# Attention weighting with the latents stationary, row sums on GpSimd, and queries placed by DMA in a transformer-layer kernel

## The chip, the cores and the metric

The kernel runs on one core of a Trainium2 chip. The metric is device time in microseconds, the median of several executions, lower is better. One further execution was recorded by the hardware profiler; durations of single instructions come from it. TensorE is PE in the rows (PEld its weight loads), VectorE is DVE, ScalarE is ACT, GpSimd is POOL and SyncE, which only issues DMAs here, is SP.

## The reference

The layer takes x of shape (16, 512, 256), 16 sequences of 512 tokens, and returns x plus an attention output plus a feed-forward output, both computed from the normalised x. Cut to what matters:

```
xn = (x - mean) / sqrt(var + 1e-5)
q = (xn @ Wq.T)                                  # 8 heads of 64
kv_latent = xn @ Wkv_down.T                      # 64 wide
k, v = kv_latent @ Wk_up.T, kv_latent @ Wv_up.T  # 8 heads of 64
attn = softmax(q k^T / 8);  a = (attn @ v) @ Wo.T
gate, y = fp4_linear(xn, w_gate), fp4_linear(xn, w_up)   # 704 wide
f = fp4_linear(silu(gate) * y, w_down)
return x + a + f
```

`fp4_linear` rounds both operands in blocks of 16 to a grid of eight magnitudes, scaled by the largest magnitude of the block. All numbers are float32 and every result must be close to float32.

## The kernel before, in words

Weights are folded once: Wk_up into Wq (`wqk`), Wv_up into Wo (`wov`). Each head then works on the 64-wide latents themselves: the scores are folded query times latent, and the weighted sum is a sum of latents (`lat_tok`, tokens on partitions, with a column of ones behind the 64 latents in which the sum of the weights appears). Most products split each operand into a rounded float32r part and a float32r remainder and do three matmuls (`limbs`, line 774). The product of probabilities and latents is not split. It is plain float32, and the trace records each such matmul as two matmuls with a weight load each; they are called halves here. The program that is built has 2,048 of these matmuls, the trace has 4,096.

The steady part is a loop of 128 slots, one for each head of each sequence, written out by hand for each engine; LEAD slots before it prepare and quantise weights, TAIL slots after it drain. In slot t, PE does: the gate product of a 128-token chunk and half of the 704 columns into bank `m0`; two of four maxima matmuls (`mx`, query chunk against all keys) for head t+2; a transpose of the row maxima of head t+1 (line 928); the up product into `m1`; key scores of head t (`st`, two matmuls each, lines 889 and 890, the second adds the query remainder and minus the row maximum); the transposes of the quantised hidden chunk of slot t-2 (line 876); the weighting matmuls (`weigh`, line 904: probabilities of 128 keys by 128 queries as the stationary operand, 65 columns of `lat_tok` as the moving one, 16 matmuls for a head); the down product of slot t-2. Every second slot adds the folded query of a pair of heads, or the transposes of a token chunk, or of a pair of normalised head outputs (`on`, line 1016). Once in a sequence of eight slots come the latents, their transposes (line 1024), and the output product `wov` in two halves. One PSUM bank, `m2`, takes all transposes. The outputs of a head lie with queries on partitions, so DVE divides them by the sum per partition (lines 675, 680), and PE turns them afterwards.

ACT does the tanh of the gate, the exponentials (line 506, one for each 128 keys of a head), and the rounded copies out of PSUM, among them four 64-partition copies of a query pair (line 546). DVE does the row maxima (line 611), the elementwise steps of the hidden chunk, the block scales (lines 583 to 588), the power of two of each value by two bit operations (`to_grid`, lines 593 and 595), the remainders, and the sums into `acc`. POOL does three elementwise steps for each hidden chunk and each token chunk. SP issues the loads of x, the stores and one 2 KB transfer for each head. Each engine works through its own list in order and waits on semaphores, so a late instruction holds everything behind it on its engine. `QH` is 4: queries of two pairs are held at a time.

## Time and profile before

| what | us |
|---|---|
| median of 3 runs | 1689.79 |
| lowest, highest | 1688.26, 1696.55 |
| the profiled execution, its own time | 1696.03 |
| its span, first to last instruction | 1694.0 |

The page gives for each engine the time it was busy in the span. A busy PE is not PE at its peak, because matmuls overlap and their recorded ends are modelled: the distance from one start to the next tells what a matmul costs. The chain of waits goes back from the last instruction, at each step to what released it or to the instruction ahead of it on its engine; a stretch of the chain that stays on PE is one in which PE had no gap. The granted clock of PE is a share of its full clock: 1.00 is 2.4 GHz, 0.50 is 1.2 GHz.

### The profile page before, as it was taken

To read this page: it belongs to the slowest core of one execution; us is meant where nothing else is said; L and a number is where in the kernel's file an instruction comes from. 1 tells how busy PE (TensorE), PEld (TensorE's weight loads), DVE (VectorE), ACT (ScalarE), POOL (GpSimd) and SP (SyncE) were. 2 spreads that over 40 slices of the span, in tenths; PEclk is the share of its full clock that TensorE was granted. 3 is DMA by queue.
4 is the path that set the end of the run, shared out by engine and by line. 5 is a ranking of instruction groups with operands and counts; after the bars stand their busy time and mean duration, and the time that the engine had idled before them with its cause. 6 is when DMAs were issued, how large, how long until landed. Compare 5 with 4: busy or idle time off the path is not lost.

```text
span 1694.0 us, 30412 instructions
## 1 busy us (share of the span) xinstructions
PE 1577.0 (93%) x10726; PEld 1442.1 (85%) x10726; DVE 1340.1 (79%) x3368; ACT 708.9 (42%) x1382; POOL 517.8 (31%) x696
## 2 busy tenths in 40 slices
PE   0599999999999999999999999999999999999998
PEld 0488998989889898988989899898989989898897
DVE  8788787888888888888878788878888877787663
ACT  2444444444444444444443444444344444344432
POOL 7433232332232233323223323223233322332211
PEclk9799999999999999999999999999999999999999
DMA  3000000000000000000000000000000000000000
GB/s 98 7 10 4 8 20 4 19 8 11 14 8 17 7 20 7 10 14 7 17 7 20 4 14 14 8 17 7 20 5 14 14 4 20 7 11 8 1 14 13
DMA packets 22885, 22.60 MB, mean 13 GB/s; under 512 B 3280, under 2 KB 22224, under 8 KB 22736
## 3 DMA queue, kind: packets, MB, share of 16 engines
q1 hardware_dynamic: 22736, 20.65, 4.0%
q8 instruction: 89, 1.46, 0.4%
q14 instruction: 60, 0.49, 0.1%
HBM read 11.99 MB, written 8.39 MB: 12 GB/s over the span
## 4 chain that ended last, share of the span: by engine, by line
PE 87%; DVE 9%; issue 3%; ACT 1%; DMA 0%; POOL 0%; SPq 0%; DVEq 0%; POOLq 0%
PE m L774 35%; PE po L904 23%; PE mx L863 7%; PE st L889 7%; PE st L890 6%; PE m L876 3%; PE m L1010 2%; PE m L1016 1%; PE m L928 1%; DVE row_max L611 1%; PE m L1024 1%; DVE hid L595 1%; DVE on_lo L745 1%; DVE h_small L583 1%; DVE x_small L583 1%
## 5 line engine op out<-in xcount | busy, mean ns | idle before, releaser
L904 PEld LDWEIGHTS po<-lat_tok,probs 128*128 128x128 f32 x4096 | 523.5, 194 | 22.9
L904 PE MATMUL po<-lat_tok,probs 128*128 128x65 f32 x4096 | 519.1, 270 | 0.0
L506 ACT ACTIVATE probs<-st 128x512 f32<-128x512 f32 x512 | 291.3, 595 | 338.2 <-PE st L890 338.2
L611 DVE TENSOR_REDUCE row_max<-mx 128x1 f32<-128x512 f32 x512 | 327.7, 682 | 0.6 <-PE mx L863 0.6
L411 POOL TENSOR_TENSOR h_norm<-hid,h_small 128x352 f32<-128x352 f32 x128 | 100.8, 788 | 480.7 <-DVE h_small L588 480.7
L889 PE MATMUL st<-q_hi,lat 128*128 128x512 f32 x512 | 212.7, 415 | 0.0
L890 PE MATMUL st<-q_lo,lat 65*128 65x512 f32 x512 | 203.6, 398 | 0.0
L774 PE MATMUL m<-wgu_hi,xt_hi 128*128 128x352 f32 x512 | 191.9, 375 | 0.1
L724 DVE TENSOR_TENSOR q_lo<-m,q_hi 64x512 fp32r<-64x512 f32 x128 | 88.1, 688 | 122.4 <-ACT q_hi L546 122.4
L442 POOL TENSOR_TENSOR h_norm<-h_norm,hid 128x352 f32<-128x352 f32 x128 | 119.7, 935 | 211.6 <-DVE h_norm L597 211.6
L863 PE MATMUL mx<-lat,q_hi 128*128 128x512 f32 x512 | 176.5, 426 | 4.0 <-DVE row_max L611 3.9
L546 ACT ACTIVATE q_hi<-m 64x512 fp32r<-64x512 f32 x256 | 151.5, 592 | 64.0 <-PE m L774 59.3
L774 PE MATMUL m<-wgu_lo,xt_hi 128*128 128x352 f32 x512 | 169.5, 331 | 0.0
L774 PE MATMUL m<-wgu_hi,xt_lo 128*128 128x352 f32 x512 | 168.4, 329 | 0.0
L526 ACT ACTIVATE ht_hi<-m 128x384 fp32r<-128x384 f32 x128 | 62.8, 491 | 198.5 <-PE m L876 198.5
L657 DVE TENSOR_TENSOR ht_lo<-m,ht_hi 128x384 fp32r<-128x384 f32 x128 | 71.3, 557 | 67.4 <-ACT ht_hi L526 67.4
L774 PEld LDWEIGHTS m<-wgu_hi,xt_hi 128*128 128x128 f32 x512 | 100.7, 197 | 14.0 <-issue 4.6
L514 ACT ACTIVATE hid<-m 128x352 f32<-128x352 f32 x128 | 59.4, 464 | 125.1 <-PE m L774 121.7
L774 PE MATMUL m<-wd_hi,ht_hi 128*128 128x256 f32 x384 | 107.7, 280 | 1.3 <-DVE ht_lo L657 1.3
L774 PE MATMUL m<-wd_hi,ht_lo 128*128 128x256 f32 x384 | 107.0, 279 | 0.0
L774 PE MATMUL m<-wd_lo,ht_hi 128*128 128x256 f32 x384 | 106.9, 278 | 0.0
L411 POOL TENSOR_TENSOR hq<-h_norm,h_small 128x352 f32<-128x352 f32 x128 | 100.7, 787 | 10.0
(178 smaller groups left out, 3054.2 us busy)
## 6 DMA issues: line engine op xcount, KB each, us to landing
x_in<-in_L_attn_x_dram SPq DMA_DIRECT2D x64, 128.0 KB, 2.2
out_dram<-acc SPq DMA_DIRECT2D x32, 256.0 KB, 2.3
q_lo<-neg_max SPq DMA_DIRECT2D x128, 2.0 KB
weights_in<-in_L_ffn_w_down_dram SPq DMA_DIRECT2D x1, 704.0 KB, 6.3
weights_in<-in_L_ffn_w_gate_dram SPq DMA_DIRECT2D x1, 640.0 KB, 4.7
acc<-in_L_ffn_w_up_dram SPq DMA_DIRECT2D x1, 640.0 KB, 5.9
wq_in<-in_L_attn_Wq_dram SPq DMA_DIRECT2D x1, 512.0 KB, 5.9
x_in<-in_L_attn_Wo_dram SPq DMA_DIRECT2D x1, 512.0 KB, 7.0
```

The costliest lines, as they stand in the source:

```text
L411: return pool.tensor_tensor(blocks(dst), blocks(src), per_block.unsqueeze(2).broadcast_to([rows, cols // BLOCK, BLOCK]), ALU.mult)
L442: pool.tensor_tensor(h_norm[:, :], h_norm[:, :], hid[:, w.c % 2, :], ALU.subtract).then_inc(h_grid, 1)
L506: act.activation(probs[:, t.c % 2, kc, :], st[kc % 2][:, :], ACT.Exp).then_inc(exp_done, 1)
L546: act.activation(q_hi[v * R:(v + 1) * R, 2 * m.c % QH + u, :], m1[u * R:(u + 1) * R, :], ACT.Copy).then_inc(q_hi_done, 1)
L611: dve.tensor_reduce(row_max[:, u.c % 2, qc:qc + 1], mx[qc % 2][:, :], AX.X, ALU.max).then_inc(mx_taken, 1)
L657: dve.tensor_tensor(ht_lo[:, u.c % 2, :, :], m2[:, 0:NB * P].rearrange("p (k q) -> p k q", k=NB), ht_hi[:, u.c % 2, :, :].bitcast(F32), AL ...
L724: dve.tensor_tensor(q_lo[0:R, h, :], m1[v * R:(v + 1) * R, :], q_hi[v * R:(v + 1) * R, h, :].bitcast(F32), ALU.subtract).then_inc(q_lo_don ...
L774: last = pe.matmul(dst, a, b, start=(n == 0), stop=(n == len(ms) - 1))
L863: pe.matmul(mx[qc % 2][:, :], q_hi[:, u.c % QH, qc * P:(qc + 1) * P], lat[:, s.c % 2, :], start=True, stop=True).then_inc(mx_psum, 1)
L889: pe.matmul(st[kc % 2][:, :], lat[:, s.c % 2, keys], q_hi[:, h, :], start=True, stop=False)
L890: pe.matmul(st[kc % 2][:, :], lat1[:, s.c % 2, keys], q_lo[:, h, :], start=False, stop=True).then_inc(st_psum, 1)
L904: last = pe.matmul(po[:, qc * P:qc * P + R + 1], probs[:, u.c % 2, kc, qc * P:(qc + 1) * P], lat_tok[:, s.c % 2, kc, 0:R + 1], start=(kc = ...
```

## The change

- **The weighting product is turned round.** The 64 latents of 128 keys are now stationary, and the 512 probabilities of those keys for all queries stream. The two heads of a pair go to partitions 0 to 63 and 64 to 127 of `po`, that is, to two column tiles of the array. There are 8 such matmuls for a pair of heads, done together in one even slot, where there were 32 of 65 columns.
- **The sums.** GpSimd adds the probabilities of the four key chunks of a head (`add_keys`, three additions of 128x512). TensorE then multiplies the sum tiles with a column of ones: 16 matmuls for a pair, each with 64 stationary columns of the sum tile taken 8 elements apart, and one moving column. DVE takes reciprocals (128x8). They lie on other partitions than needed, so SP writes them to DRAM and reads them back spread over the partitions (`inv_b`).
- **The head outputs** come out already turned, so the transposes of `on` go. DVE scales a pair with one multiplication, ACT rounds it, GpSimd takes the remainder (before, DVE).
- **Queries.** ACT rounds a pair with one 128-partition copy and DVE takes one remainder, where there were four copies and two remainders. SP places the results with six transfers a pair.
- **Grid rounding** of the hidden and token chunks: two ACT operations (square, then a bf16 copy with a bias) replace two DVE bit operations.
- **Down product**: the two halves of a chunk accumulate in one group of 18 matmuls every second slot; x is loaded a second time, into `acc`, as what it is added to.
- **Order** within a slot is new on all engines; the latent transposes go to `m1`; LEAD has 14 slots (12), TAIL 6 (4).

The diff, cut to its core:

```
-        def turned_pair(t):
+        def weighed_pair(t):
             m = t.plus(-2).over(2)
             return m if t.c % 2 == 0 and m.within(B * PAIRS) else None
+        def scaled_pair(t):
+            m = t.plus(-3).over(2)
+            return m if t.c % 2 and m.within(B * PAIRS) else None
+        def split_pair(t):
+            return weighed_pair(t.plus(-2))
...
+        def down_chunk(t):
+            n = t.plus(-5).over(2)
+            return n if t.c % 2 and n.within(B * CH) else None
         def wov_half(t):
             s = t.over(H).plus(-1)
-            m = s.times(2, t.c % H - 1)
-            return m if t.c % H in (1, 2) and m.within(B * 2) else None
-        LEAD = [At(c) for c in range(-12, 0)]
-        TAIL = [At(SLOTS + c) for c in range(4)]
+            m = s.times(2, t.c % H - 2)
+            return m if t.c % H in (2, 3) and m.within(B * 2) else None
+        LEAD = [At(c) for c in range(-14, 0)]
+        TAIL = [At(SLOTS + c) for c in range(6)]
...
+            def place_query(m, u):
+                h = 2 * m.c % QH + u
+                sp.wait_ge(q_hi_done, m.n(1, 1))
+                if u and m.over(2).any():
+                    sp.wait_ge(st_psum, m.n(2 * CH, -2 * CH))
+                for v in range(2):
+                    sp.dma_start(q_hi[v * R:(v + 1) * R, h, :].bitcast(F32), qp_hi[u * R:(u + 1) * R, :].bitcast(F32)).then_inc(q_hi_placed[u], 16)
+                sp.wait_ge(q_lo_done, m.n(1, 1))
+                sp.dma_start(q_lo[0:R, h, :].bitcast(F32), qp_lo[u * R:(u + 1) * R, :].bitcast(F32)).then_inc(q_lo_placed[u], 16)
...
+                m = scaled_pair(t)
+                if m is not None:
+                    sp.wait_ge(inv_done, m.n(1, 1))
...
+                if m is not None:
+                    sp.wait_ge(inv_stored, m.n(16, 16))
+                    for v in range(2):
+                        sp.dma_start(inv_b[v * R:(v + 1) * R, :],
+                                     inv_rows[m.c % 2, v:v + 1, :].broadcast_to([R, T])).then_inc(inv_spread, 16)
...
+                m = q_pair(t)
+                if m is not None:
+                    place_query(m, 0)
...
+            def add_keys(t, kc):
+                total, last = key_sum[:, t.c % 2, :], probs[:, t.c % 2, kc, :]
+                pool.wait_ge(exp_done, t.n(CH, kc + 1))
+                if kc == 1:
+                    if t.over(2).any():
+                        pool.wait_ge(den_psum, t.over(2).n())
+                    first = probs[:, t.c % 2, 0, :]
+                else:
+                    pool.wait_ge(sum_step, t.n(CH - 1, kc - 1))
+                    first = total
+                pool.tensor_tensor(total, first, last, ALU.add).then_inc(sum_step, 1)
...
                 if w.within(SLOTS):
-                    pool.wait_ge(h_round, w.n(ROUND_STEPS, ROUND_STEPS))
+                    add_keys(w, 3)
+                m = split_pair(t)
+                if m is not None:
+                    pool.wait_ge(on_hi_done, m.n(1, 1))
+                    pool.tensor_tensor(on_lo[:, m.c % PAIRS, :], on[:, :], on_hi[:, m.c % PAIRS, :].bitcast(F32),
+                                       ALU.subtract).then_inc(on_lo_done, 1)
...
+                if t.within(SLOTS):
+                    add_keys(t, 1)
+                    add_keys(t, 2)
...
+                    act.wait_ge(h_norm_done, w.n(1, 1))
+                    act.activation(hid[:, w.c % 2, :], h_norm[:, :], ACT.Square, scale=MAGIC_SQUARE).then_inc(h_square, 1)
+                    act.wait_ge(h_square, w.n(1, 1))
+                    act.activation(h_magic[:, :], hid[:, w.c % 2, :], ACT.Copy, bias=MAGIC_LEAST).then_inc(h_magic_done, 1)
+                n = norm_chunk(w)
...
+                m = split_pair(t)
+                if m is not None:
...
+                m = q_pair(t)
+                if m is not None:
...
-                m = q_pair(t)
-                if m is not None:
-                    act.wait_ge(q_psum, m.n(1, 1))
-                    if m.any(2 * CH, -2 * CH):
-                        act.wait_ge(st_psum, m.n(2 * CH, -2 * CH))
-                    for u in range(2):
...
+                max_rows(t, 0)
+                max_rows(t, 1)
...
+                m = scaled_pair(t)
+                if m is not None:
+                    dve.wait_ge(inv_spread, m.n(32, 32))
+                    dve.wait_ge(pv_done, m.n(CH, CH))
+                    if m.any():
+                        dve.wait_ge(on_hi_done, m.n())
+                        dve.wait_ge(on_lo_done, m.n())
+                    dve.tensor_tensor(on[:, :], po[:, :], inv_b[:, :], ALU.mult).then_inc(on_done, 1)
+                m = q_pair(t)
+                if m is not None:
+                    dve.wait_ge(q_hi_done, m.n(1, 1))
...
+                m = weighed_pair(t)
+                if m is not None:
+                    dve.wait_ge(den_psum, m.n(1, 1))
+                    if m.any(1, -1):
+                        dve.wait_ge(inv_stored, m.n(16, -16))
...
-            def weigh(t, n):
-                u, kc = (t.plus(-1), n + 2) if n < 2 else (t, n - 2)
-                if u.within(SLOTS):
-                    s = u.over(H)
-                    if kc == 0:
-                        if u.any():
-                            pe.wait_ge(on_done, u.n())
-                        pe.wait_ge(ltok_done, s.n(1, 1))
-                    pe.wait_ge(exp_done, u.n(CH, kc + 1))
-                    for qc in range(CH):
-                        last = pe.matmul(po[:, qc * P:qc * P + R + 1], probs[:, u.c % 2, kc, qc * P:(qc + 1) * P],
-                                         lat_tok[:, s.c % 2, kc, 0:R + 1], start=(kc == 0 and qc == 0),
-                                         stop=(kc == CH - 1), skip_group_check=True)
...
+            def weigh(t):
+                m = weighed_pair(t)
+                if m is not None:
+                    s = m.over(PAIRS)
+                    if m.any():
+                        pe.wait_ge(on_done, m.n())
+                    pe.wait_ge(ltok_done, s.n(1, 1))
+                    for kc in range(CH):
+                        pe.wait_ge(exp_done, m.n(2 * CH, CH + kc + 1))
+                        for v in range(2):
+                            last = pe.matmul(po[v * R:(v + 1) * R, :], lat_tok[:, s.c % 2, kc, 0:R], probs[:, v, kc, :],
+                                             start=(kc == 0), stop=(kc == CH - 1))
+                        last.then_inc(pv_done, 1)
...
+            def weights_sum(t):
+                m = weighed_pair(t)
+                if m is not None:
+                    s = m.over(PAIRS)
+                    if t.plus(-2).within(SLOTS) or t.plus(1).within(SLOTS):
+                        turned_taken(t)
+                    else:
+                        m2_free(t.plus(-1))
+                    pe.wait_ge(sum_step, m.n(2 * (CH - 1), 2 * (CH - 1)))
+                    for j in range(T // R):
+                        for v in range(2):
+                            last = pe.matmul(m2[v * R:(v + 1) * R, j:j + 1],
+                                             key_sum[:, v, :].rearrange("p (q j) -> p q j", j=T // R)[:, :, j],
+                                             lat_tok[:, s.c % 2, 0, R:R + 1], start=True, stop=True)
+                    last.then_inc(den_psum, 1)
...
-                                           wgu_lo[:, k, cols]) for k in range(KD)]).then_inc(up_psum, 1)
+                if wov_half(t.plus(-1)) is None:
+                    gate(t)
+                    up(t)
+                else:
+                    up(t)
+                    gate(t)
+                turn(t)
+                weigh(t)
                 key_scores(t, 0)
-                turn_hidden(t)
-                weigh(t, 0)
                 key_scores(t, 1)
-                weigh(t, 1)
+                if q_pair(t) is not None:
...
-                                       for k in range(NB)]).then_inc(down_psum, 1)
+                weights_sum(t)
                 key_scores(t, 2)
                 key_scores(t, 3)
```

What TensorE's list has between the transposes of a hidden chunk and the next maxima matmuls, before (in the program itself; each `po` row stands for twice as many records of the trace):

```order
L876 MATMUL m<-ident,hq 128x128 x3
L904 MATMUL po<-lat_tok,probs 128x65 x4
L889 MATMUL st<-q_hi,lat 128x512
L890 MATMUL st<-q_lo,lat 128x512
L904 MATMUL po<-lat_tok,probs 128x65 x4
L863 MATMUL mx<-lat,q_hi 128x512 x2
```

And in an even slot of the changed kernel (`m` of line 1052 is bank m2):

```order
L987 MATMUL m<-ident,hq 128x128 x3
L991 MATMUL m<-ident,row_max 4x128
L1036 MATMUL po<-probs,lat_tok 64x512 x8
L1003 MATMUL st<-q_hi,lat 128x512
L1004 MATMUL st<-q_lo,lat 128x512
L1003 MATMUL st<-q_hi,lat 128x512
L1004 MATMUL st<-q_lo,lat 128x512
L975 MATMUL mx<-lat,q_hi 128x512 x2
L1052 MATMUL m<-lat_tok,key_sum 64x1 x16
```

The four weighting groups of every slot have become one group of eight long matmuls in every second slot, and the 16 short ones stand behind the maxima.

SP's list over three slots, before:

```order
L384 DMA out_dram<-acc 128x2x256
L376 DMA q_lo<-neg_max 1x4x128
L384 DMA out_dram<-acc 128x2x256
L351 DMA x_in<-in_L_attn_x_dram 128x256
L376 DMA q_lo<-neg_max 1x4x128 x2
```

And now, over an even and an odd slot:

```order
L423 DMA q_lo<-neg_max 1x4x128
L453 DMA acc<-in_L_attn_x_dram 128x256
L419 DMA inv_rows<-inv_den 128x8
L423 DMA q_lo<-neg_max 1x4x128
L428 DMA inv_b<-inv_rows 64x512 x2
L409 DMA q_hi<-qp_hi 64x512 x2
L411 DMA q_lo<-qp_lo 64x512
L382 DMA x_in<-in_L_attn_x_dram 128x256
L409 DMA q_hi<-qp_hi 64x512 x2
L411 DMA q_lo<-qp_lo 64x512
```

The store and the two spreads of the reciprocals stand round the transfer of the negated maxima, ahead of the queries.

GpSimd's list over one slot, before:

```order
L442 TENSOR_TENSOR h_norm<-h_norm,hid 128x352
L411 TENSOR_TENSOR hq<-h_norm,h_small 128x352
L458 TENSOR_TENSOR rstd<-rstd,minus_half 128x1
L411 TENSOR_TENSOR h_norm<-hid,h_small 128x352
L411 TENSOR_TENSOR x_norm<-xn,x_small 128x256
```

And now, in an even slot:

```order
L516 TENSOR_TENSOR key_sum<-key_sum,probs 128x512 x2
L526 TENSOR_TENSOR on_lo<-on,on_hi 128x512
L533 TENSOR_TENSOR h_norm<-h_norm,h_magic 128x352
L481 TENSOR_TENSOR hq<-h_norm,h_small 128x352
L549 TENSOR_TENSOR rstd<-rstd,minus_half 128x1
L481 TENSOR_TENSOR h_norm<-hid,h_small 128x352
L481 TENSOR_TENSOR x_norm<-xn,x_small 128x256
L516 TENSOR_TENSOR key_sum<-probs 128x512
```

Key sums and a remainder of 512 columns have come in around the steps of the hidden chunk.

## Rows read from the trace of the kernel before

**Rows 1.** The page's part 1: span, busy time and share, instructions

```profile
span 1694.0 us, 30412 instructions
PE 1577.0 (93%) x10726; PEld 1442.1 (85%) x10726; DVE 1340.1 (79%) x3368; ACT 708.9 (42%) x1382; POOL 517.8 (31%) x696
```

**Rows 2.** The page's part 4: the chain that ended last, by engine

```profile
PE 87%; DVE 9%; issue 3%; ACT 1%; DMA 0%; POOL 0%; SPq 0%; DVEq 0%; POOLq 0%
```

**Rows 3.** Line 514, the tanh, one for each slot: min/median/max ns, first and last start

```profile
L514 ACT ACTIVATE hid<-m x128: 459/464/467, 91.5 to 1664.7; 128x352 f32<-128x352 f32 x128
```

**Rows 4.** The chain, 800 to 826 us: start us, length us, what

```profile
800.24 1.40 PE m L774 x6
...
806.64 1.02 PE m L774 x6
807.65 0.46 PE mx L863 x2
808.11 0.11 PE m L928
808.22 0.96 PE m L774 x6
...
809.42 0.23 PE st L890
...
812.69 1.06 PE m L774 x9
...
814.69 0.84 PE po L904 x8
815.53 2.79 PE m L774 x24
818.32 0.44 PE m L1016 x4
```

**Rows 5.** The timeline, PE, 96 to 98 us: start, length, what

```profile
96.14 1.90 PE L904 MATMUL po<-lat_tok,probs 128*128 128x65 f32 x16
97.84 0.41 PE L774 MATMUL m<-wgu_hi,xt_hi 128*128 128x352 f32 x1
```

**Rows 6.** The timeline, PE, 53.5 to 57 us: plain float32, 256 columns

```profile
53.59 1.92 PE L822 MATMUL st<-weights_in 128*128 128x256 f32 x4
55.30 1.91 PE L822 MATMUL po<-weights_in 128*128 128x256 f32 x4
```

**Rows 7.** Busy time by stretches: PE, PEld, DVE, ACT, POOL, then PE clock

```profile
53.40:57.00 3.60, 3.60 (x10) 2.79 (x9) 1.05 (x2) 1.19 (x2) 1.07 (x2) 0.50 0.00 0
93.00:140.00 47.00, 45.77 (x304) 41.02 (x303) 43.23 (x108) 21.17 (x42) 16.44 (x22) 1.00 0.02 7
90.00:890.00 800.00, 769.99 (x5274) 704.99 (x5274) 653.58 (x1641) 345.17 (x669) 242.19 (x322) 0.99 0.04 11
```

**Rows 8.** The chain, 800 to 899 us: pieces that are not PE's work

```profile
866.49 0.61 DVE on_lo L745
...
884.53 0.43 issue
```

**Rows 9.** Lines 442 and 451, POOL, two inputs from SBUF: min/median/max ns

```profile
L442 POOL TENSOR_TENSOR h_norm<-h_norm,hid x128: 925/932/952, 100.3 to 1671.4; 128x352 f32<-128x352 f32 x128
L451 POOL TENSOR_TENSOR x_norm<-x_norm,xq x64: 722/733/752, 14.3 to 1526.8; 128x256 f32<-128x256 f32 x64
```

**Rows 10.** Groups of instructions by line: busy us, mean ns | idle before

```profile
L724 DVE TENSOR_TENSOR q_lo<-m,q_hi 64x512 fp32r<-64x512 f32 x128 | 88.1, 688 | 122.4 <-ACT q_hi L546 122.4
L595 DVE TENSOR_SCALAR hid<-hid 128x352 f32<-128x352 f32 x128 | 66.6, 520 | 4.4
L546 ACT ACTIVATE q_hi<-m 64x512 fp32r<-64x512 f32 x256 | 151.5, 592 | 64.0 <-PE m L774 59.3
```

**Rows 11.** DMA issues (KB each, us to landing) and SP's queue in the timeline

```profile
x_in<-in_L_attn_x_dram SPq DMA_DIRECT2D x64, 128.0 KB, 2.2
...
821.53 0.58 SPq L376 DMA_DIRECT2D q_lo<-neg_max  x1
```

More of the change, by code:

```diff
@@ L208, in transformer_layer @@
         q_lo_done = sem("q_lo_done")
+        q_hi_placed = [sem(f"q_hi_placed{b}") for b in range(2)]
+        q_lo_placed = [sem(f"q_lo_placed{b}") for b in range(2)]
         mx_psum = sem("mx_psum")
@@ L236, in transformer_layer @@
         down_taken = sem("down_taken")
+        res_loaded = [sem(f"res_loaded{c}") for c in range(CH)]
         wov_psum = sem("wov_psum")
@@ L327, in lead_work @@
         def lead_work(t):
-            i = t.c + len(LEAD)
+            i = t.c + 12
+            if i < 0:
+                return range(0), range(0)
             quants = (min(2 * i, len(WQUANT)), min(2 * i + 2, len(WQUANT)))
@@ L553, in slot @@
                                    ACT.Copy).then_inc(xt_hi_done, 1)
-                m = turned_pair(t)
-                if m is not None:
-                    act.wait_ge(on_psum, m.n(1, 1))
-                    if m.over(PAIRS).any(2):
-                        act.wait_ge(wov_psum, m.over(PAIRS).n(2))
-                    act.activation(on_hi[:, m.c % PAIRS, :], m2[:, :], ACT.Copy).then_inc(on_hi_done, 1)
                 s = ltok_seq(t)
@@ new lines, in slot @@
+                if m is not None:
[9 more added lines that the diff above has]
+                    if m.any():
+                        for u in range(2):
+                            dve.wait_ge(q_lo_placed[u], m.n(16))
+                    dve.tensor_tensor(qp_lo[:, :], m1[:, :], qp_hi[:, :].bitcast(F32), ALU.subtract).then_inc(q_lo_done, 1)
@@ L909, in slot, with into_hidden @@
[L909 to L920 removed]
+            def into_hidden(t, dst, first, done):
+                s, c, j = t.over(H), t.c % H // 2, t.c % 2
+                b, tok, cols = s.c % 2, slice(c * P, (c + 1) * P), slice(first + j * HALF, first + (j + 1) * HALF)
+                limbs(dst[:, 0:HALF], [(xt_hi[:, b, KD + k, tok], xt_lo[:, b, KD + k, tok], wgu_hi[:, k, cols],
+                                        wgu_lo[:, k, cols]) for k in range(KD)]).then_inc(done, 1)
@@ L944, in slot @@
+                m = q_pair(t)
+                if m is not None:
+                    b, cols = m.over(PAIRS).c % 2, slice(m.c % PAIRS * P, (m.c % PAIRS + 1) * P)
+                    limbs(m1[:, :], [(wqk_hi[:, k, cols], wqk_lo[:, k, cols], xt_hi[:, b, k, :], xt_lo[:, b, k, :])
+                                     for k in range(KD)]).then_inc(q_psum, 1)
+                d = down_chunk(t)
+                if d is not None:
                     if t.within(SLOTS):
```

345 lines of the change are left out of this document (171 added, 174 removed).

## The prediction

> **What bounds the kernel now.** I read the page's part 1 first: PE is busy for 93% of the span, DVE for 79%, POOL for 31% [rows 1]. A busy share of PE proves little, so the chain of waits came next: 87% of it is PE, 9% DVE [rows 2], and most of that 9% is the preparation before the first slot. The tanh is done once in each slot, so its first and last start give the period: (1664.7 - 91.5) / 127 = 12.39 us a slot [rows 3]. Between 800 and 826 us the chain does not leave PE at all [rows 4]. So the slots are bound by how long TensorE takes for its list; gaps come in a few places.
>
> How much is list and how much is gap, for a pair of slots (24.77 us)? From the pieces of the chain [rows 4]: four gate and up products of about 1.0 are 4.0; eight maxima matmuls at 0.23 are 1.9; sixteen score matmuls at 0.235 are 3.8; eight single transposes at 0.11 are 0.9; eight weighting groups at 0.84 are 6.7; two down products 2.1; a query product 1.4; two groups of four transposes 0.9. A sequence of four pairs adds two output products of 2.8, and the latents and their transposes (1.4 and 0.44), 1.9 for a pair. The sum is 23.6. So 1.2 us of a pair are gaps. Two of them show: DVE's work for the transpose bank `m2` before the latents can be turned, and short waits ahead of the row maxima [rows 8].
>
> **What a plain float32 matmul costs.** This decides everything. At the 1.2 GHz level (granted clock 0.50 [rows 7]) four halves of 256 columns take 55.30 - 53.59 = 1.71 us [rows 6], 0.428 each, which is 513 clocks: a half streams a column in two clocks. At 2.4 GHz (clock 1.00 [rows 7]) sixteen halves of 65 columns take 97.84 - 96.14 = 1.70 us [rows 5], 0.106 each, while 65 columns would stream in 0.054. So the weighting matmuls of before are bound by what comes with a half, the load of 128 stationary columns, and not by streaming.
>
> **The change, part by part**, for a pair of slots.
> - Weighting, removed: 64 halves at 0.105 = -6.7 us. Transposes of `on`, removed: -0.44 [rows 4].
> - Weighting, added: 8 matmuls, 16 halves of 512 columns. Each streams 1024 clocks, 0.427 us at 2.4 GHz; the float32r matmuls of 512 columns take 0.235 [rows 4] where 512 clocks are 0.213, 10% more, so the bounds are 0.427 and 0.47, and I take 0.45. The load is hidden behind the stream. No row shows two column tiles at work. If the tiles do not overlap, all 16 halves stand in a row: 7.2 us. If they overlap, the order is two halves on tile A, two on tile B; the second half of one runs beside the first of the other, and the group takes 9 halves: 9 x 0.45 = 4.05. I take 4.05 and keep 7.2 for the range. The Trainium skill says in "TensorEngine Tiling (Array Packing)", section Key Properties, that different tiles can load weights and multiply in parallel, and that a change of the tiling mode drains the engine; no run so far shows the first here.
> - Mode changes, added: four for a pair. The nearest row is the transpose with four stationary columns between 128-wide ones, 0.11 like other transposes [rows 4], so nothing to 0.3 us each; I take 0.3 in all.
> - Sums of the weights, added: 16 matmuls, 32 halves with 64 stationary columns and one moving column. No row shows one. From above the half with 128 stationary columns bounds it, 0.106: 3.4 us. From below, if the two tiles load side by side, a quarter: 0.8. Half the columns at the same rate are 0.053; with something for issue I take 0.06, 1.9 us.
> - Gaps: the latents' transposes leave `m2`, the transposes of `on` are gone, and the row-maxima transpose comes after gate and up; the waits of [rows 8] go. What is late next is DVE in the odd slot: it must wait for the spread reciprocals, scale the pair, take the query remainder and the down product, and only then does the maxima 2 and 3 which the next slot's first matmuls need. I let 0.6 of the 1.2 us remain; bounds 0 and 1.8.
> - POOL: two-input steps take 0.932 for 352 and 0.733 for 256 columns [rows 9], 2.07 ns a column, so 512 columns take 1.26. Three key sums a slot and half a remainder are 4.4 us beside the 242.19 / 800 x 12.39 = 3.75 of now [rows 7]: 8.2 us of a slot of 11.6. That hides, and it costs if the slot falls under 8.2 or each addition grows above 2.2 us.
> - DVE: 653.58 / 800 x 12.39 = 10.1 us a slot now [rows 7]. It loses the bit operations (line 595 alone 0.52 [rows 10]), one of two query remainders (0.69 a pair [rows 10]), the remainder of `on` (0.61 [rows 8]), the small division. Some 2 us less a slot, none of it directly on the path, since PE was.
> - ACT: 345.17 / 800 x 12.39 = 5.3 us now. Four query copies of 0.592 [rows 10] become one; up to 1.4 us of squares and copies come in. It stays under 6.2 us, hidden.
> - SP: nine more issues for a pair, and one load of 128 KB again. At 0.58 an issue [rows 11] about 13 issues take 7.5 us of 23, hidden in bulk. In order it matters: the spread waits behind the negated maxima, which appear about 3.3 us into the odd slot. Two issues (1.2) and a landing like that of x (2.2 [rows 11]) give 6.7 us; DVE, by its list, comes there at about 6.8. The queries' first half must be there at the next slot's start: rounded at about 6, placed at 9.3, in a slot of about 11. Both are close and cost nothing as long as a small DMA lands in about 2 us.
>
> The sum for a pair: -6.7 - 0.44 + 4.05 + 0.3 + 1.9 - 0.6 = -1.5 us, from 24.8 to 23.3. Times 64: -96 us. TAIL has the store and the spread on its path, LEAD two more slots in which nothing waits: +4 (0 to 10). Against the profiled execution, 1696.0 - 96 + 4 = 1604. That execution was 6.2 us above the median of the runs, so the median should be about 1598; I say 1600.
>
> **The rivals.**
> - *The column tiles do not overlap.* The group takes 16 halves, 7.2 us, and the pair grows by 3.15: +202 us, of which the longer even slot gives DVE and SP time and hides perhaps 10. About 1790, slower by 6%. Its place is line 1036, and it decides as soon as the group takes over 5.6 us (4.05 + 1.5). For it: no row of before shows overlap, and two streams of float32 must be read at once. Against it: each half takes a column only every second clock, so both together need no more than one float32r stream reads.
> - *The small loads are slow.* The sums' stationary tile is read 8 elements apart. If this halves the rate of the load, a half costs 0.106 as with 128 columns, the sums take 3.4 us and not 1.9: +96, about 1695, no change to slightly slower. Every stationary operand in the rows is read without a step, so they neither exclude nor show it. The same holds if 0.106 is the cost of issue and not of 128 columns. The Trainium skill's "SBUF — State Buffer", section Door 1, has the rule that speaks for it: lines of 16 bytes, and a penalty for each access that moves to a new line, which 32-byte steps always do.
> - *The reciprocals come late.* DVE waits in every odd slot for the DRAM round trip. Each microsecond beyond 6.8 us into the slot delays query remainder, down product and maxima, and so the next slot: 64 us for each. With landings of 3 us instead of 2.2, on the store and on the spread, about +1: 1665. For it: SP issues in order behind two waits. Against it: the store is issued early in the slot, well before the maxima.
>
> **How the numbers follow.** Forecast 50% (1600, its own range 1545 to 1665), tiles apart 24% (about 1790), slow loads 16% (about 1695), late reciprocals 10% (about 1665). What this measurement can tell from no change is about 0.5%, 8 us. Faster by more: nearly all of the forecast, a quarter of the slow loads, two thirds of the late reciprocals, 0.58. Within it 0.07. Slower: the tiles apart, half of the slow loads, 0.35. The range runs from 1545 to 1790; it holds the first, third and fourth case and half of the second.
>
> **What would show it.** In the changed profile the eight matmuls of line 1036 should lie 0.85 to 0.95 us apart for a pair of heads and the group should hold PE for about 4 us; 7 us means that the tiles stand in a row. Line 1052's 32 halves should take about 2 us; 3.4 means slow loads. The tanh's period should be near 11.65 us. DVE should wait little for `inv_b` at line 793. POOL should be near 70% busy and not appear on the chain. The forecast is wrong if the chain runs through POOL or SP, or if line 1036 takes more than 5.6 us.

## The result and the profile after

The changed kernel takes 1681.51 us (median of 8 runs, 1671.57 to 1689.08) against 1691.01 us for the kernel before on the same chip (8 runs); the ratio is 0.994, 95% interval 0.9914 to 0.9966. I had forecast 1600 us. The measured time lies in the range, but of a gain of 91 us only about 10 came. The profiled execution took 1683.32 us, with a span of 1681.5.

The page's parts 1, 2 and 4 of the changed kernel:

```profile
span 1681.5 us, 28756 instructions
...
PE 1561.3 (93%) x9446; PEld 1217.2 (72%) x9446; DVE 1167.5 (69%) x2664; ACT 716.8 (43%) x1574; POOL 1068.4 (64%) x1144
...
PEclk9689999999999999999999999999989999998998
...
PE 71%; DMA 9%; DVE 7%; ACT 5%; issue 3%; SPq 3%; POOL 1%; POOLq 0%; DVEq 0%; ACTq 0%
PE m L875 28%; PE po L1036 13%; PE mx L975 8%; PE m L1052 8%; DMA inv_b<-inv_rows 6%; PE st L1003 6%; PE st L1004 4%; DMA q_hi<-qp_hi 3%; PE m L987 2%; DVE qp_lo L800 1%; SPq L423 1%; DVE row_max L717 1%; SPq L428 1%; ACT probs L602 1%; ACT neg_max L618 1%
```

Against [rows 1] PE is as busy as before, 93%, with 1280 fewer matmul records and 225 us less weight loading. A list that I reckoned 1.5 us a pair shorter keeps the engine busy for nearly as long. Against [rows 2] the chain has a new part, DMA 9% and SP's queue 3%, where both were 0%. So there are two places to look for the lost gain: why TensorE needs so long for a shorter list, and what the transfers hold up.

The tanh of each slot, line 610 now (first and last start at the end of the times):

```profile
L610 ACT ACTIVATE hid<-m x128: 463/463/467, 96.5 to 1646.7; 128x352 f32<-128x352 f32 x128
```

The period is (1646.7 - 96.5) / 127 = 12.21 us, where [rows 3] gave 12.39 and I expected 11.65. A pair of slots takes 24.41 us: 0.36 less than before, not 1.5 less.

The chain of waits of the changed kernel over a pair (start us, length us, what):

```profile
787.63 0.64 SPq L423
...
788.32 0.51 SPq L428
...
788.88 2.96 DMA inv_b<-inv_rows
...
791.87 0.06 DVE on L793
...
792.47 0.68 DVE qp_lo L800
...
797.60 3.58 PE po L1036 x16
...
802.78 2.02 PE m L1052 x32
...
805.93 4.37 PE m L875 x24
...
814.70 4.17 DMA inv_b<-inv_rows
```

Read it from its three ends. The 16 halves of line 1036 hold PE for 3.58 us: the column tiles do overlap. The 32 halves of the sums take 2.02. And then, behind four score matmuls, the output product, 24 matmuls of 256 columns, takes 4.37 us, where the same product took 2.79 in [rows 4] (the row at 815.53). Nothing in its instructions has changed. In the timeline of PE its matmuls start 0.12 us apart, then 0.21, then 0.12 again:

```profile
802.71 2.09 PE L1052 MATMUL m<-lat_tok,key_sum 128*64 128x1 f32 x32
...
805.89 0.28 PE L875 MATMUL m<-wov_lo,on_hi 128*128 128x256 f32 x1
806.00 0.28 PE L875 MATMUL m<-wov_hi,on_lo 128*128 128x256 f32 x1
...
807.11 0.41 PE L875 MATMUL m<-wov_hi,on_lo 128*128 128x256 f32 x1
807.32 0.41 PE L875 MATMUL m<-wov_hi,on_hi 128*128 128x256 f32 x1
...
809.77 0.28 PE L875 MATMUL m<-wov_hi,on_hi 128*128 128x256 f32 x1
809.89 0.28 PE L875 MATMUL m<-wov_lo,on_hi 128*128 128x256 f32 x1
```

The windows of the same kernel (busy time of PE, PEld, DVE, ACT, POOL, then the granted clock) show why. The second stretch ends with the score matmuls, the third holds most of the output product:

```profile
802.00:806.00 4.00, 4.00 (x42) 3.40 (x41) 2.37 (x7) 1.47 (x4) 2.01 (x3) 1.00 0.01 1
806.00:810.00 4.00, 4.00 (x23) 4.00 (x22) 0.29 (x3) 0.58 (x2) 3.28 (x4) 0.57 0.01 0
810.00:816.00 6.00, 5.65 (x32) 4.72 (x31) 4.35 (x8) 3.23 (x9) 1.74 (x2) 1.00 0.05 17
...
100.00:1600.00 1500.00, 1451.15 (x8854) 1129.67 (x8853) 1062.98 (x2388) 655.35 (x1438) 977.68 (x1023) 0.94 0.23 59
```

The burst of short matmuls ends at 804.8. From about 806.2 on the clock is at 0.50, the 1.2 GHz level, for 3.4 us, and PE is busy all the time. Over 100 to 1600 us the mean is 0.94. The kernel before in the same stretch:

```profile
100.00:1600.00 1500.00, 1449.73 (x9940) 1329.74 (x9939) 1210.98 (x3026) 642.13 (x1244) 448.26 (x592) 0.98 0.04 11
```

A mean of 0.98 is 1500 x 0.02 x 2 = 60 us at the lower level, 0.94 is 180 us. Of the 120 us more, half is lost, since each microsecond there does half the work: about 60 us (the two decimals leave it open by 15 or so).

Not every burst does this. The trace of the changed kernel has 61 bursts between 100 and 1600 us and 45 falls of the clock. Of these, 38 begin between 0.5 us before and 1.7 us behind the end of a burst, with no gap of TensorE over 0.15 us in the 8 us ahead of them; they hold 147 of the 171 us at the lower level. The other seven begin around 2 us behind the start of an idle stretch of 1.3 to 2.1 us. The kernel before has nine falls over the same stretch, and all nine stand at such an idle stretch (1.4 to 2.1 us, TensorE waiting for DVE ahead of the transposes of the latents), as here, with columns as above:

```profile
865.00:866.00 1.00, 0.01 (x1) 0.00 (x0) 0.93 (x3) 0.60 (x1) 0.62 (x1) 1.00 0.00 0
866.00:867.00 1.00, 0.00 (x0) 0.00 (x0) 1.00 (x2) 0.00 (x0) 0.43 (x1) 0.74 0.00 0
867.00:868.00 1.00, 0.85 (x4) 0.86 (x5) 0.09 (x1) 0.00 (x0) 0.92 (x2) 0.50 0.00 0
```

So the clock falls here behind two different things: a wait of TensorE, and a burst of short matmuls during which it counts as busy.

The waits of the changed kernel on the new transfers and the new tilings (total us, times, longest), and the landings of its DMAs (KB each, us):

```profile
PEld po L1036 <- issue: 123.6, 447, 0.3
...
PEld st L1003 <- issue: 51.3, 64, 0.8
...
PEld mx L975 <- DMA q_hi<-qp_hi: 41.2, 43, 2.4
...
DVE on L793 <- DMA inv_b<-inv_rows: 26.1, 34, 2.3
```

```profile
q_hi<-qp_hi SPq DMA_DIRECT2D x256, 128.0 KB, 2.3
...
inv_b<-inv_rows SPq DMA_DIRECT2D x128, 128.0 KB, 2.9
...
inv_rows<-inv_den SPq DMA_DIRECT2D x64, 4.0 KB, 1.4
```

### The profile page after: what moved, and what is told of

The parts are those of the page before. It is cut to its first block, busy times and chain, and to the rows that moved or that the text cites. A ratio compares the mean times of both kernels' runs of the same rounds, so it can differ in the third digit from the quotient of the medians.

```text
span 1681.5 us, 28756 instructions
## 1 busy us (share of the span) xinstructions
PE 1561.3 (93%) x9446; PEld 1217.2 (72%) x9446; DVE 1167.5 (69%) x2664; ACT 716.8 (43%) x1574; POOL 1068.4 (64%) x1144
## 3 DMA queue, kind: packets, MB, share of 16 engines
q8 instruction: 77, 1.26, 0.3%
## 4 chain that ended last, share of the span: by engine, by line
PE 71%; DMA 9%; DVE 7%; ACT 5%; issue 3%; SPq 3%; POOL 1%; POOLq 0%; DVEq 0%; ACTq 0%
PE m L875 28%; PE po L1036 13%; PE mx L975 8%; PE m L1052 8%; DMA inv_b<-inv_rows 6%; PE st L1003 6%; PE st L1004 4%; DMA q_hi<-qp_hi 3%; PE m L987 2%; DVE qp_lo L800 1%; SPq L423 1%; DVE row_max L717 1%; SPq L428 1%; ACT probs L602 1%; ACT neg_max L618 1%
## 5 line engine op out<-in xcount | busy, mean ns | idle before, releaser
L516 POOL TENSOR_TENSOR key_sum<-key_sum,probs 128x512 f32<-128x512 f32 x256 | 329.2, 1286 | 38.7 <-ACT probs L602 2.5
L1036 PE MATMUL po<-probs,lat_tok 128*64 128x512 f32 x1024 | 233.8, 598 | 0.0
L533 POOL TENSOR_TENSOR h_norm<-h_norm,h_magic 128x352 f32<-128x352 f32 x128 | 112.0, 875 | 154.7 <-DVE h_norm L774 154.7
L526 POOL TENSOR_TENSOR on_lo<-on,on_hi 128x512 fp32r<-128x512 f32 x64 | 82.8, 1293 | 196.2 <-ACT on_hi L643 196.2
L516 POOL TENSOR_TENSOR key_sum<-probs 128x512 f32<-128x512 f32 x128 | 163.5, 1277 | 8.9 <-PE m L1052 8.9
L1036 PEld LDWEIGHTS po<-probs,lat_tok 128*64 128x64 f32 x1024 | 67.8, 136 | 123.9 <-issue 123.6
L975 PEld LDWEIGHTS mx<-lat,q_hi 128*128 128x128 f32 x512 | 96.1, 204 | 82.9 <-DMA q_hi<-qp_hi 41.2
L1003 PEld LDWEIGHTS st<-q_hi,lat 128*128 128x128 f32 x512 | 100.7, 197 | 69.6 <-issue 51.3
L1052 PEld LDWEIGHTS m<-lat_tok,key_sum 128*64 128x64 f32 x2048 | 128.3, 216 | 24.6 <-issue 24.6
L1052 PE MATMUL m<-lat_tok,key_sum 128*64 128x1 f32 x2048 | 133.6, 259 | 0.9 <-POOL key_sum L516 0.9
L1004 PEld LDWEIGHTS st<-q_lo,lat 65*128 65x128 f32 x512 | 102.6, 200 | 14.9
```

Of the source, the lines that this page charges most:

```text
L516: pool.tensor_tensor(total, first, last, ALU.add).then_inc(sum_step, 1)
L526: pool.tensor_tensor(on_lo[:, m.c % PAIRS, :], on[:, :], on_hi[:, m.c % PAIRS, :].bitcast(F32), ALU.subtract).then_inc(on_lo_done, 1)
L533: pool.tensor_tensor(h_norm[:, :], h_norm[:, :], h_magic[:, :], ALU.subtract).then_inc(h_grid, 1)
L975: pe.matmul(mx[qc % 2][:, :], q_hi[:, u.c % QH, qc * P:(qc + 1) * P], lat[:, s.c % 2, :], start=True, stop=True).then_inc(mx_psum, 1)
L1003: pe.matmul(st[kc % 2][:, :], lat[:, s.c % 2, keys], q_hi[:, h, :], start=True, stop=False)
L1004: pe.matmul(st[kc % 2][:, :], lat1[:, s.c % 2, keys], q_lo[:, h, :], start=False, stop=True).then_inc(st_psum, 1)
```

## The experiments

Ratios are to the kernel before, run on the same chip, with their 95% intervals. The clock is the mean of the granted clock over 100 to 1600 us unless another stretch is named.

| kernel | us | ratio | clock |
|---|---|---|---|
| before | 1691.01 | 1 | 0.98 |
| changed | 1681.51 | 0.994 (0.9914 to 0.9966) | 0.94 |
| one of eight sum columns | 1503.56 | 0.8885 (0.8859 to 0.8911) | 1.00 (to 1500) |
| sums in four groups | 1676.15 | 0.9899 (0.9849 to 0.995) | 0.97 |
| spread issued first | 1647.75 | 0.9721 (0.9678 to 0.9763) | 0.95 |
| before, with a burst | 1926.19 | 1.1377 (1.1307 to 1.1447) | 0.92 |
| spread first, head 0 direct | 1649.91 | 0.9777 (0.9732 to 0.9821) | 0.93 (span) |
| ones stationary | 1615.61 | 0.9554 (0.954 to 0.9568) | 0.98 |
| four groups, spread first | 1657.28 | 0.9803 (0.9777 to 0.9828) | 0.97 (to 1500) |
| both heads on one tile | 1897.85 | 1.121 (1.1169 to 1.1251) | 0.94 (span) |
| ones stationary, reciprocal last | 1655.45 | 0.9813 (0.9784 to 0.9841) | 0.96 |
| ones stationary, in two halves | 1588.83 | 0.9422 (0.94 to 0.9445) | 0.99 |

**Is it the burst's own time or what it does to the clock?** Two kernels, one that takes the burst away and one that puts it elsewhere. The first computes one of the eight sum columns and leaves out the other seven, so the normalisation is not the reference's; all else stays.

```
-                    for j in range(T // R):
+                    for j in range(1):
...
-  dve.reciprocal(inv_den[:, m.c % 2, :], m2[:, 0:T // R])
+  dve.reciprocal(inv_den[:, m.c % 2, :], m2[:, 0:1].broadcast_to([P, T // R]))
```

> The changed kernel with 1 of the 8 columns of the sum matmuls (4 halves in place of 32; the reciprocals take that column 8 times, so the normalisation is left out). List theory: TensorE loses 28 halves of 0.063 us, 1.77 us a pair, 64 pairs: -113 us from 1681, about 1568. Clock theory: the burst of short matmuls is also what lowers TensorE's clock to the 1.2 GHz level for some 3.4 us in every second pair; then the granted clock rises from 0.93 to about 0.97 and another 60 us go: about 1508. If a wait behind the DRAM trip bounds the pair, less than 113 goes: above 1568.

Measured 1503.56. 28 of 32 halves are gone, 28 x 2.02 / 32 = 1.77 us a pair, 113 us in all. The gain is 178 us, so 65 us are not the burst's own time. That is less than the windows give: a mean of 0.94 over 1500 us is 90 us lost, this kernel loses under 10, and so some 80 came back. The rest may be waits that the lower clock had covered, or the two decimals; the runs do not tell. A window of this kernel shows the clock that came back:

```profile
700.00:1000.00 300.00, 291.02 (x1641) 219.88 (x1640) 245.82 (x556) 149.61 (x331) 227.50 (x237) 1.00 0.26 68
```

The second takes the kernel before and adds 32 halves of the same shape, on constant data and into unused columns of `m2`, in every second slot; nothing waits for their results.

```
+                    if t.c % 2 == 0:
+                        for n in range(8):
+                            for v in range(2):
+                                pe.matmul(m2[v * R:(v + 1) * R, NB * P + n:NB * P + n + 1],
+                                          x_const[:, v, :].rearrange("p (q j) -> p q j", j=8)[:, :, n],
+                                          ident[:, 0:1], start=True, stop=True)
```

> The kernel before with 16 idle plain float32 matmuls added in every second slot ahead of the down product, 64 stationary columns taken 8 apart and one moving column, results unused (the burst of the change, measured by itself in a list without other changes). List theory: 32 halves of 0.063 us and 0.3 for the change of tiling, 2.3 us a pair, +148 us: about 1838 and a mean clock of 0.97 as before. Clock theory: the clock falls behind the burst here too, another +60: about 1900, clock near 0.93.

Measured 1926.19. The burst in its chain, and one window of it:

```profile
801.38 2.02 PE m L956 x32
```

```profile
400.00:700.00 300.00, 292.77 (x2060) 268.17 (x2059) 207.34 (x525) 109.35 (x211) 77.86 (x103) 0.91 0.03 10
```

The list grows by 64 x 2.02 = 129 us, and the kernel before took 1694.44 on this chip, which makes 1824. The other 102 us are more than the list: over 100 to 1800 the mean of the clock is 0.924 (0.91 to 0.93 up to 1600 us, 0.96 behind that), 1700 x 0.076 = 129 us lost, less the 30 of before, 99. So the burst lowers the clock in a kernel that has nothing else of the change, and two different ways of counting agree within a few microseconds. Together with the kernel above this settles that the burst is the cause.

**Can the burst be spread out?** The eight columns in four groups of two, between the scores and the maxima:

```
                weigh(t)
+                weights_sum(t, 0)
                key_scores(t, 0)
                key_scores(t, 1)
+                weights_sum(t, 1)
...
-                weights_sum(t)
+                weights_sum(t, 2)
                key_scores(t, 2)
                key_scores(t, 3)
+                weights_sum(t, 3)
```

> The changed kernel with the 16 sum matmuls in four groups of four: behind the weighting group, behind key scores 1, behind the maxima matmuls, behind key scores 3. Same matmuls, same results. Clock theory: fewer stretches of short matmuls at once, the clock falls less often, -60 us, against which two or three more changes of the tiling stand with 0.3 us each for a pair, +40 to +50: about 1670, mean clock above 0.96. If the clock has another cause: clock unchanged at 0.93 and 1720 to 1730.

Measured 1676.15, with the changed kernel's interval overlapping. The clock rose from 0.94 to 0.97, as the theory of the clock wanted, which is 1500 x 0.03 = 45 us given back, and the time hardly moved. I had expected 1670 for this case, with a price of 40 to 50 us for more changes of the tile size. The first group stands behind the weighting group, which has the same tile size; each of the other three has a change ahead of it and one behind it. The waits show the place:

```profile
L1053 PEld LDWEIGHTS m<-lat_tok,key_sum 128*64 128x64 f32 x2048 | 148.8, 210 | 104.3 <-issue 104.3
```

The load sat idle 104.3 us ahead of the sums with the cause "issue", against 24.6 us in the changed kernel. Idle time of the load is not all lost, so this shows the place and a bound, not the sum; that the changes of tile size take the rest of the 45 us is argued.

**What does the late spread cost?** In SP's order the two spread transfers go ahead of the maxima's transfer, which waits for ACT:

```
+                if m is not None:
+                    sp.wait_ge(inv_stored, m.n(16, 16))
+                    for v in range(2):
+                        sp.dma_start(inv_b[v * R:(v + 1) * R, :], ...)
                 u = t.plus(1)
                 if u.within(SLOTS):
                     sp.wait_ge(neg_done, u.n(1, 1))
```

> The changed kernel with SP's two issues that spread the reciprocals moved ahead of the transfer of the negated maxima. Queue theory: the spread lands up to 2 us earlier in each odd slot, DVE's scaling and with it query remainder, down product and maxima are earlier; 1.0 to 1.5 us of a pair go, -64 to -96 us, about 1600. Clock theory alone: the gaps are covered anyway, -20 us or less, about 1665. If the negated maxima become late instead: no gain.

Measured 1647.75: 34 us less than the changed kernel, so the late spread was worth that much. In this kernel it is gone:

```profile
DVE on L792 <- DMA inv_b<-inv_rows: 3.5, 1, 3.5
```

It lies between the two expectations, 1600 and 1665, with the clock still at 0.95. Its chain shows what is late next, the rounded query behind ACT's work for the other streams:

```profile
823.87 0.50 ACT qp_hi L653
...
824.38 0.50 SPq L409
...
824.93 2.33 DMA q_hi<-qp_hi
...
827.30 0.94 PE mx L974 x2
```

So I let ACT write head 0's rounded query straight from PSUM into `q_hi`, and dropped its two transfers, on top of this order:

```
+  for v in range(2):
+      act.activation(q_hi[v * R:(v + 1) * R, 2 * m.c % QH, :], m1[0:R, :], ACT.Copy).then_inc(q_direct, 1)
...
-  for v in range(2):
+  for v in range(2 if u else 0):
```

> e3 (1648 us) and, for the first head of a pair, ACT writes the rounded query straight from PSUM in two 64-partition copies; only the second head's goes by DMA. In e3 the chain takes 6.9% in the landing of q_hi. Theory that the trip of the query is the next wait: its issue 0.5 and landing 2.3 go, two copies of 0.59 come, about 1 to 1.5 us in those odd slots that wait: -40 to -70, about 1595. Rival, ACT is late itself (its squares stand ahead of the exponentials) and the two copies delay the next exponentials: -10 or a loss.

Measured 1649.91, no gain. DMA and SP's queue left the chain (9% together with the spread in front, 0% now); in their place ACT went from 10% to 13%, DVE from 4% to 7% and issue from 3% to 5%. The expectation's rival, that ACT is late itself and two more copies delay it, fits, but the chain is that of the slowest execution, 1664.95, and no run holds ACT's delay alone.

The spread in front and the sums in four groups together:

> e2 and e3 together: the sum matmuls in four groups, the spread issued first. If the two causes are separate their gains add: 1681 - 33 - 5, about 1642. If a steadier clock only moves work into the waits of the odd slots, e3's gain grows with it, since with the spread early nothing is left to cover: 1600 to 1620.

Measured 1657.28. The gains do not add; the two together are slower than the spread alone, although the clock is at 0.97 and not at 0.95. What costs more than the clock gives back was not measured by itself; the three extra groups and their changes of tile size are all that differs.

**Do the two column tiles really run together?** Both heads go to column tile 0, head 1 on top of head 0, so that the weighted sums of the two heads are mixed; the instructions are the same in number and size.

```
-  last = pe.matmul(po[v * R:(v + 1) * R, :], ..., start=(kc == 0), stop=(kc == CH - 1))
+  last = pe.matmul(po[0:R, :], ..., start=(kc == 0 and v == 0), stop=(kc == CH - 1 and v == 1))
```

> The changed kernel with both heads' weighting matmuls on column tile 0 (their sums run together, the second tile's output is left out). Measures the overlap of the tiles. If the tiles overlap as the trace says (3.65 us for 16 halves), this takes 16 x 0.43 = 6.9 us a group: +3.2 us a pair, +205 us, about 1885, less what gaps absorb (up to 30) and less if the longer streaming holds the clock up. If the overlap in the trace is only in the modelled ends: no change.

Measured 1897.85. The group, in the chain:

```profile
812.57 7.01 PE po L1036 x16
```

7.01 us against 3.58, and (7.01 - 3.58) x 64 = 220 us against 216 measured. The overlap is nearly complete: a half is 0.438, and 16 of them on two tiles take the time of 8.2.

**Another way to the same sums.** A block of ones is stationary and the key sums are streamed, 4 halves of 512 columns for a pair; each of 64 rows then holds the sum, so the trip through DRAM goes, but DVE takes a reciprocal of 128x512.

```
-  for j in range(T // R):
-      for v in range(2):
-          last = pe.matmul(m2[v * R:(v + 1) * R, j:j + 1], key_sum[...][:, :, j], lat_tok[..., R:R + 1], ...)
+  for v in range(2):
+      last = pe.matmul(m2[v * R:(v + 1) * R, :], ones_w[:, :], key_sum[:, v, :], start=True, stop=True)
...
-  dve.reciprocal(inv_den[:, m.c % 2, :], m2[:, 0:T // R]).then_inc(inv_done, 1)
+  dve.reciprocal(inv_b[:, :], m2[:, :]).then_inc(inv_done, 1)
```

> The changed kernel with the sums taken by ones as the stationary operand (64 columns) and the summed probabilities streamed, 2 matmuls of 512 columns on the two column tiles, so that the sums come out spread over the partitions: no short matmuls, no DRAM trip; DVE takes one reciprocal of 128x512 in an even slot in place of 128x8. TensorE: 3 halves' time of 0.4 in place of 2.0, -50 us; clock theory: no fall behind it, -60; no wait for the spread, -30. DVE's reciprocals show about 5.9 ns a column beyond a base (0.207 us at 8, 0.289 at 22), so 512 columns would take about 3.1 us. If that hides on DVE (69% busy): about 1550. If DVE then bounds the pair, 1600 to 1680.

Measured 1615.61. The clock is back at 0.98. The reciprocal takes 3.36 us, which is 6.6 ns a column:

```profile
L806 DVE RECIPROCAL inv_b<-m 128x512 f32<-128x512 f32 x64 | 214.9, 3358 | 5.7 <-PE m L1042 5.7
```

DVE is now busy for 85% of the span and has 21% of the chain. Two orders on DVE followed. In the first the whole reciprocal stands behind the next chunk's scales and the latents' low part:

```
-  (weighed_pair) dve.reciprocal(inv_b[:, :], m2[:, :])      # ahead of xn and its scales
+  (weighed_pair) dve.reciprocal(inv_b[:, :], m2[:, :])      # behind lat
```

> As the streamed-ones kernel (1615.6 us), but VectorE's reciprocal of 128x512 stands behind the scales of the next x chunk and the low limb of the latents in its slot, not ahead of them. There the chain of waits of the streamed-ones kernel holds it: 3.13 us from 806.95 and then VectorE up to the latents' limb at 811.4. If it is the order on VectorE that costs, some 1 us of each 25 us pair comes back in the slots where the latents or the x chunk are waited for: about 1570 to 1600 us. Rival: VectorE is simply full (85% busy), so whatever stands last is late, and the turning of the next slot now waits for the reciprocal: 1610 to 1640 us.

Measured 1655.45: slower than either of the two expectations. It is the rival's mechanism at a higher price: the load and the transposes of the next slot wait for the bank that the reciprocal reads.

```profile
PEld m L978 <- DVE inv_b L824: 62.3, 34, 4.3
```

Part of the price is the clock, though this kernel has no burst of short matmuls. The kernel with ones stationary and this one, over the same stretch:

```profile
100.00:1600.00 1500.00, 1392.47 (x7439) 1007.91 (x7437) 1302.57 (x2456) 678.21 (x1490) 1023.12 (x1058) 0.98 0.20 49
100.00:1600.00 1500.00, 1385.19 (x7261) 1003.27 (x7259) 1240.45 (x2416) 662.65 (x1455) 993.40 (x1033) 0.96 0.20 49
```

The 0.02 are about 30 of the 40 us between them. All 24 falls of this kernel begin within 4.2 us of the start of an idle stretch of TensorE of 2.0 to 2.4 us.

In the second it is cut in two: 256 columns in the old place, 256 behind the latents' low part.

> As the one before, but the reciprocal is cut into two pieces of 256 columns, one in its old place and one behind the latents' limb. If order is what costs, it lands between: about 1590 to 1610 us; if the total of VectorE is the bound, it is no faster than 1615 us, plus about 0.1 us a pair for the second instruction, 6 us.

Measured 1588.83, the fastest of all and just ahead of what was expected, with the clock at 0.99:

```profile
L806 DVE RECIPROCAL inv_b<-m 128x256 f32<-128x256 f32 x64 | 112.5, 1758 | 5.7 <-PE m L1049 5.7
L831 DVE RECIPROCAL inv_b<-m 128x256 f32<-128x256 f32 x64 | 109.4, 1710 | 0.5
```

The second instruction costs (1758 + 1710 - 3358) = 110 ns, and the order gives back 27 us in all, 22 by the ratios. Other cuts were not tried.

## Why the prediction was wrong, step by step

- **What bounds the kernel.** Right: the slots were bound by TensorE's list, and the list of the changed kernel can still be counted from the same rows.
- **The tiles, "I take 4.05 and keep 7.2 for the range".** Right in kind, and a little too dear: 3.58 to 3.65 us instead of 4.05, 26 to 30 us in all in favour of the change. The experiment with one tile shows that the overlap is worth 216 us.
- **The sums, 1.9 us a pair.** Right: 2.02 to 2.09. The small loads are not slow; with a step of 8 elements in the stationary operand a half still takes 0.063 us, against 0.106 for 128 columns [rows 5]. The Trainium skill's "SBUF — State Buffer", section Door 1, which stood beside the rival of slow loads, has lines of 16 bytes and a penalty for each access that moves to a new one. By it a half would cost more than with adjacent elements; no row here has both, so a small price is not excluded. Half of 0.106 is 0.053, so it would be at most 0.01 us a half.
- **The failed step is the sum itself: "-6.7 - 0.44 + 4.05 + 0.3 + 1.9 - 0.6 = -1.5 us".** Every term of it takes the 2.4 GHz level for granted. I had used both levels to price a half [rows 6, 7], and then assumed that PE, always busy, would stay at the upper one. It does not: behind 2 us of matmuls with one moving column the clock fell in 38 of 61 pairs, mostly for 3.4 us. On average this takes about 1 us of each pair: 60 us in all against the kernel before by the windows, and the kernel with one sum column got 65 us back beyond its list. The term was put at nothing without a reason, and no rival held it. The forecast of the period was 23.3 us a pair and it came out at 24.4; the clock is the largest part of the difference.
- **"Both are close and cost nothing as long as a small DMA lands in about 2 us".** Wrong for the spread: it landed in 2.9 us, and in 4.17 in the next pair, not in 2.2, and SP took it up only behind the maxima's transfer; DVE stood idle for it in 34 of the 64 pairs, 0.8 us each time. This is my third rival, to which I gave 10%. It costs 34 us, and the order on SP's queue removes it. The rounded queries are late too (41.2 us of waits of the load, 3% of the chain), and they become the next wait when the spread is on time. My sign of being wrong, a chain through SP, came true.
- **Gaps, 0.6 us of a pair left.** Too small. With the spread and the queries the chain spends 9% in DMA and 3% in SP's queue. The gaps of before, too, were not all waits: at a clock of 0.98 about 0.5 of the 1.2 us are the lower level, which the sum did not name. The 123.6 us of issue waits ahead of line 1036 (447 of them, 0.28 each) lie beside the other tile's work and cost little: the group takes 3.58 us with them. The 51.3 us ahead of line 1003 (64 of them, 0.8 each) fit the tile size changing back behind the sums. In the timeline the first score matmul behind the weighting group (801.11) and the one behind the sums (804.73) are each followed by the next after 0.34 us, where the later ones of these groups stand 0.23 apart, so on PE's own path a change behind a group cost little here.
- **Tail and lead, +4 us.** The first tanh starts 5.0 us later than in [rows 3], and behind the last one there are 34.8 us instead of 29.3: +10.5, just above my bounds of 0 to 10.
- **POOL 8.2 us a slot, 70% busy.** Nearly: 64% busy, the key sums 1.28 us each where I took 1.26, 1% of the chain, on which it was not to appear. DVE (69% busy) and ACT (43%) have room as reckoned, but ACT is now 5% of the chain, where it was 1%.

Together, from 1600: the clock about +60, the spread +34, tail and lead +6.5, the cheaper weighting -28, and the sum of the small ones +10 makes 1682. The last is what is left over, and since the gains do not add (a lower clock hides part of a late transfer), the parts should not be read finer than some 15 us.

What stays open: why a burst of this kind brings the clock down while PE counts as busy, and why 23 of the 61 bursts did not. The experiments show that it does, in two kernels, and that with the same sums as matmuls of 512 columns all falls but those at idle stretches are gone. The groups of halves with 65 moving columns in the kernel before brought no fall by themselves. What lies between one column and 65 was not measured.

## What to carry to other kernels

Before pricing a list of matmuls at the full clock, ask whether the change makes a stretch of PE's work out of very short ones; compare the granted clock before and after over the same stretch, and look at it right behind the new work. A wait of TensorE costs more than its length where the clock falls behind it, as in the kernel with the reciprocal last. Do a small reduction with the roles of its operands swapped, so that the long operand streams, even if this computes each result many times. And where a queue is served in order, price its transfers with the wait of the instruction ahead of them, not by their landing alone; a long instruction on a nearly full engine is worth cutting so that its neighbours can pass between the pieces.

## What the runs showed of the hardware beyond that

- Two column tiles with plain float32 and 512 moving columns run side by side at almost full rate: 16 halves in 3.58 us, against 7.01 on one tile.
- DVE's short instructions became longer beside the busier POOL. Line 691, a scale of 22 columns, means 512 ns now; the same work at line 585 took 190 before. The sum of variance and epsilon, one column, went from 165 to 397 ns, and the rounding of x from 460 (line 597) to 881.

The changed kernel:

```profile
L691 DVE TENSOR_SCALAR h_small<-h_small 128x22 f32<-128x22 f32 (+2 forms) x136 | 69.7, 512 | 4.7
L778 DVE TENSOR_TENSOR x_norm<-x_norm,x_magic 128x256 f32<-128x256 f32 x64 | 56.4, 881 | 14.1 <-ACT x_magic L635 13.5
L749 DVE TENSOR_TENSOR rstd<-mean_var,rstd 128x1 f32<-128x1 f32 x64 | 25.4, 397 | 2.2
```

The kernel before:

```profile
L597 DVE TENSOR_TENSOR x_norm<-x_norm,xq 128x256 f32<-128x256 f32 x64 | 29.4, 460 | 2.2
L585 DVE TENSOR_SCALAR h_small<-h_small 128x22 f32<-128x22 f32 (+2 forms) x136 | 25.8, 190 | 4.6
L643 DVE TENSOR_TENSOR rstd<-mean_var,rstd 128x1 f32<-128x1 f32 x64 | 10.5, 165 | 2.2
```

The Trainium skill's "SBUF — State Buffer", section Who interferes with whom, says that a DVE instruction with two inputs from SBUF contends with a GpSimd instruction that reads SBUF. The trace of the changed kernel agrees for the two additions with two inputs. Where POOL is idle, line 749 takes 158 to 160 ns and line 778 takes 411 to 426; where POOL is at work for over half of the instruction, they mean 513 and 937. The same split holds in the kernel before (160 and 272 ns at line 643), which is nearly always in the first case. Line 691 is not of the form that the sentence names, a scale with one input, and it is split in the same way: 167 to 177 ns and 497. The row maxima, which read PSUM, take 681 ns either way. No experiment took POOL's work away alone. In this kernel the longer instructions cost little, since DVE is 69% busy.
